# Handing buffers over between the stages of a graph network kernel: first attention started from the counting buffers

## The reference

```python
# layer 0: dot-product attention over the edges, 4 heads of 64
scores = sum(q[dst] * k[src]) / 8
alpha  = softmax of scores over the edges of each dst
x = layernorm(layernorm((segment_sum(alpha * v[src]) + skip) @ Wout + x) * g + b + x)
# layer 1: GAT, 4 heads, with self loops, then a feed-forward part
e = leaky_relu(al_src[src] + al_dst[dst], 0.2)
y = layernorm(x + segment_sum(softmax(e) * h[src])) * g1 + b1
x = layernorm(layernorm(y + gelu(y @ W1) @ W2) * g2 + b2 + x)
# layer 2: two rounds of x + segment_sum(relu(x)[src]), each with a two-layer MLP
# layer 3: a GCN sum with degree norms, then GAT attention with one head, layernorm
```

## Time and profile before

| what | value |
|---|---|
| median of 3 runs | 3881.09 us (3879.44 to 3882.41) |
| the profiled execution, as timed | 3878.65 us |
| its span | 3876.9 us |
| PE busy | 3705.8 us (96%) |
| DVE busy | 2282.5 us (59%) |
| ACT busy | 2042.2 us (53%) |
| POOL busy | 534.9 us (14%) |
| counting | up to about 509 us |
| first attention | about 509 to 1625 us |
| second attention | about 1625 to 2517 us |
| sums and last attention | from about 2517 us |

### The profile page before, as it was taken

One profiled execution on the slowest core, in us unless ns is written; L12 is line 12 of the kernel. 1 busy time (PEld: TensorE's weight loads), 2 busy tenths in 40 slices (PEclk: granted clock), 3 DMA queues, 4 the chain that ended last, 5 costly groups with the idle time before them and its releaser, 6 DMA issues. The chain is left out here.

```text
span 3876.9 us, 69921 instructions
## 1 busy us (share of the span) xinstructions
PE 3705.8 (96%) x27529; PEld 2886.1 (74%) x27530; DVE 2282.5 (59%) x4502; ACT 2042.2 (53%) x3736; POOL 534.9 (14%) x599
## 2 busy tenths in 40 slices
PE   6999969999999999699999999799999999999999
PEld 3666647677777676587777777688888888888887
DVE  8999936555655655499999999600012221005665
ACT  3555546666666666499999999600001110003554
POOL 1000000111111111100005667500000000000000
PEclk9999979999999999899999999999999999999999
DMA  2555572332333233533343333154343333334332
GB/s 95 226 229 210 237 243 85 110 112 91 114 99 104 91 115 104 145 132 116 120 173 104 113 113 111 60 211 147 129 145 138 138 137 126 136 120 144 138 138 72
DMA packets 177941, 520.61 MB, mean 134 GB/s; under 512 B 54385, under 2 KB 142454, under 8 KB 144502
## 3 DMA queue, kind: packets, MB, share of 16 engines
q1 hardware_dynamic: 175110, 509.49, 37.8%
q10 hardware_dynamic: 2544, 7.08, 0.6%
HBM read 354.22 MB, written 162.29 MB: 133 GB/s over the span
## 5 line engine op out<-in xcount | busy, mean ns | idle before, releaser
L1858 PE MATMUL t_acc<-t_r,t_ct 128*128 128x256 f32 (+1 forms) x3750 | 856.0, 380 | 20.0 <-DMA t_r<-d_r 16.2
L1036 ACT ACTIVATE a_sm<-a_p_t 128x1024 f32<-128x1024 f32 (+1 forms) x800 | 669.4, 837 | 372.9 <-PE a_p_t L974 356.6
L1858 PEld LDWEIGHTS t_acc<-t_r,t_ct 128*128 128x128 f32 x3750 | 701.4, 190 | 114.1 <-DMA t_r<-d_r 16.6
L974 PE MATMUL a_p_t<-ident,a_sm 128*128 128x128 f32 x5000 | 702.8, 280 | 36.6 <-ACT a_sm L1036 20.2
L1030 ACT ACTIVATE a_sm<-a_sm,a_negm 128x1024 f32<-128x1024 f32 (+2 forms) x600 | 703.1, 1172 | 43.1 <-DVE a_negm L1098 42.8
L974 PEld LDWEIGHTS a_p_t<-ident,a_sm 128*128 128x128 f32 x5000 | 562.5, 143 | 212.9 <-issue 194.1
L988 PE MATMUL a_p_o<-a_sm,a_v 128*64 128x128 f32 x10000 | 700.6, 279 | 10.2 <-ACT a_sumT L1043 9.1
L988 PEld LDWEIGHTS a_p_o<-a_sm,a_v 128*64 128x64 f32 x10000 | 555.8, 137 | 188.1 <-issue 109.9
L1118 DVE CUSTOM_DVE_ANT_0 a_sm<-a_p_s,sh_rows 128x400 f32<-128x400 f32 x800 | 427.2, 571 | 426.8 <-PE a_p_s L960 415.2
L960 PE MATMUL a_p_s<-sh_a_bc,a_q 64*128 64x400 f32 x1600 | 397.8, 557 | 27.7 <-DMA sh_rows<-d_logs 21.7
L1139 DVE SCALAR_TENSOR_TENSOR a_sm<-sh_a_bc,sh_al 128x3125 f32<-128x3125 f32 x100 | 346.2, 3462 | 15.0 <-PEq L52 11.6
(11 more groups left out here) (248 smaller groups left out, 3682.2 us busy)
## 6 DMA issues: line engine op xcount, KB each, us to landing
t_ct<-d_ct SPq DMA_DIRECT2D x74, 1600.0 KB, 6.6
sh_rows<-d_full SPq DMA_DIRECT2D x50, 1600.0 KB, 7.1
d_logs<-logs SPq DMA_DIRECT2D x25, 1664.0 KB, 7.0
sh_rows<-d_logs SPq DMA_DIRECT2D x25, 1664.0 KB
d_ct<-ct SPq DMA_DIRECT2D x25, 1600.0 KB, 5.3
d_full<-sh_rows SPq DMA_DIRECT2D x25, 1600.0 KB, 6.3
t_ct<-d_full SPq DMA_DIRECT2D x25, 1600.0 KB, 6.8
t_x<-d_x SPq DMA_DIRECT2D x75, 128.0 KB, 6.6
```

Source lines behind the costliest of these rows:

```text
L974: m = nc.tensor.transpose(p_t[u % 2][:, i * P:(i + 1) * P], sm[buf][:, a * P:(a + 1) * P], ident[:, :])
L1036: nc.scalar.activation(sm[buf][:, a_row[u] * P:a_row[u + 1] * P], p_t[u % 2][:, 0:turns[u] * P], ACT.Copy).then_inc(s_copy, 1)
L1858: m = self.nc.tensor.matmul(self.acc[t % 2][:, 0:width], self.ct[t % 3][:, a * P:(a + 1) * P], rows[:, a, 0:width], start=a == 0, stop=a = ...
```

## The change

- `Shared` is made once, ahead of counting, and holds one wide buffer. Counting writes its counts and edges there, the first attention has its keys there, the second its source terms, and the sums their messages, counts row 2 and weights. `logs` are the two `rows` of the attentions.
- The first attention takes its tiles in the order 23, 24, 0, 1, ... 22 (`tile_at`). The logarithms of tiles 23 and 24 aren't stored and loaded; they are used where counting left them. DVE masks those of tile 23 at the end of counting.
- SP loads the keys of the first 23 tiles (eight DMAs) and the query of tile 23 (four) in the last counting tile, ahead of the store of its counts, and the keys of the last two tiles (four DMAs) behind the loop. PE waits for them in the new block, not SP in the old one.
- The scores of the first two units go round three pairs of banks: `p_s` and the two transposition buffers. The first transposition waits until all of them are masked. ACT takes one exponential ahead of its first unit.
- The source terms of the first attention's last two tiles are stored in tiles 2 and 3 of the second attention. `hand_sources` loads its first part in two pieces.
- In `post_a1` the steps with g2 and be2 move from POOL to DVE. The relu of the last five tiles writes straight into the messages of the sums; messages of the first 20 tiles and counts rows 0 to 2 are loaded within the second attention, behind its last tile. The end of that block no longer waits for stores.

```diff
+def tile_at(j):
+    return (j + NT - 2) % NT
+KEPT = 20
...
+        wide = sb("wide", [P, MESSAGES + 2 * NPAD])
+        self.a_bc = wide[:, 0:4 * NPAD].rearrange("p (h k n) -> p h k n", h=2, k=2)
+        self.messages = wide[:, 0:MESSAGES].rearrange("p (a n) -> p a n", a=NT)
+        self.kt = wide[:, 2 * NPAD:4 * NPAD].rearrange("p (h n) -> p h n", h=H0)
...
-        ct = [sb(f"ct{i}", [P, NT, P], FP32) for i in range(2)]
-        logs = [sb(f"logs{i}", [P, ROW], FP32) for i in range(2)]
+        ct, logs = shared.counts, shared.rows
...
+                def hand_keys(a, b):
+                    proj.stored_keys(sp, b)
+                    for h in range(H0):
+                        rows = w_kt[(h % 2) * HD:(h % 2 + 1) * HD, h // 2, :, :].rearrange("p j n -> p (j n)")
+                        for r in range(2):
+                            lo, hi = max(a * P, r * HALF_K), min(b * P, (r + 1) * HALF_K)
+                            if lo < hi:
+                                sp.dma_start(shared.kt[r * HD:(r + 1) * HD, h, lo - r * HALF_K:hi - r * HALF_K], rows[:, lo:hi]).then_inc(shared.s_kt, 16)
...
+                    if last:
+                        hand_keys(0, NT - 2)
+                        proj.stored_keys(sp, NT - 1)
+                        hand_queries()
                     wait_alone(sp, s_group_out, (j + 1) * GPT)
...
-                store_logs(NT - 2, 1)
                 proj.store_vs(sp, NT - 1)
-                store_logs(NT - 1, 0)
+                hand_keys(NT - 2, NT)
...
+                dve.wait_ge(s_tbank_out, (NT - 1) * NTU)
+                for e in range(NFULL):
+                    v.scalar_tensor_tensor(logs[1][:, c], logs[1][:, c], STEEP, logs[1][:, c], ALU.mult, ALU.min).then_inc(shared.s_full, 1)
...
+        def score_bank(n, i):
+            if n >= len(first_units):
+                return p_s[i % 2][:, 0:SW]
+            pair = (n * SU + i) // 2 % RING
+            return p_s[i % 2][:, 0:SW] if pair == 0 else p_t[pair - 1][:, o:o + SW]
...
-                        freed = n * SU + i - 1
+                        freed = n * SU + i - (1 if n >= len(first_units) else 2 * RING - 1)
...
+                    if dot and n == 0 and u == 0:
+                        pe.wait_ge(s_sfree, len(first_units) * SU)
...
-                    P_.store(sp, NT - 2, 1, (NT - 2) // 2)
+                    P_.store_rows(sp, NT - 2, 1, (NT - 2) // 2)
+                    P_.store_values(sp, NT - 2, 1, (NT - 2) // 2)
...
+                    if p == 0 and j in (2, 3):
+                        sp.dma_start(al_src_dram[:, :, c * P:(c + 1) * P].rearrange("h k p -> p (h k)"), shared.as_[i][:, :], allow_slow_non_contiguous=True).then_inc(shared.s_terms[i], 16)
...
-                P_.stored(sp)
+                    if j == NT:
+                        sp.wait_ge(s_mask, units - heads)
+                        sp.dma_start(shared.rows[0][:, 0:NPAD], row(ct_dram, 0)).then_inc(shared.s_sum[0], 16)
+                        sp.wait_ge(s_lift, units)
+                        sp.dma_start(shared.messages[:, 0:KEPT, :], r2_dram[:, 0:KEPT, :]).then_inc(shared.s_messages, 16)
+                        sp.wait_ge(s_mask, units)
+                        sp.dma_start(shared.rows[1][:, 0:NPAD], row(ct_dram, 1)).then_inc(shared.s_sum[1], 16)
+                        sp.dma_start(shared.row2, row(ct_dram, 2)).then_inc(shared.s_sum[2], 16)
...
                 if (lag, s) == (4, 0):
+                    v.scalar_tensor_tensor(t[:, :], t[:, :], n2.mv[:, 0:1], rows["g2"][:, :], ALU.subtract, ALU.mult).then_inc(DL.sem, 1)
+                    dve.wait_ge(DL.sem, DL.at(jj, "gain2"))
                     dve.wait_ge(PL.sem, PL.at(jj, "rstd2"))
-                    v.tensor_scalar(z[:, :], t[:, :], n2.mv[:, 0:1], n2.rs[:, 0:1], ALU.subtract, ALU.mult).then_inc(DL.sem, 1)
+                    v.scalar_tensor_tensor(z[:, :], t[:, :], n2.rs[:, 0:1], rows["be2"][:, :], ALU.mult, ALU.add).then_inc(DL.sem, 1)
...
-                    pool.tensor_tensor(z[:, :], z[:, :], rows["g2"][:, :], ALU.mult).then_inc(PL.sem, 1)
-                    pool.tensor_tensor(z[:, :], z[:, :], rows["be2"][:, :], ALU.add).then_inc(PL.sem, 1)
...
+                    to = r2[tp] if jj < KEPT else messages[:, jj, :]
+                    nc.scalar.activation(to[:, 0:D], x2[tp][:, :], ACT.Relu).then_inc(AR.sem, 1)
...
-        for i in range(NT // PIECE):
-            a = i * PIECE
-            sp.dma_start(self.ct[0][:, a * P:(a + PIECE) * P], self.ct_dram[0, :, a * P:(a + PIECE) * P]).then_inc(self.s_first[i], 16)
-            sp.dma_start(self.r[0][:, a:a + PIECE, :], self.r2[:, a:a + PIECE, :]).then_inc(self.s_first[i], 16)
         load_x(0)
         gin_weights(0)
-        load_row(1)
-        load_row(2)
```

More of the change, by code:

```diff
@@ L702, in attend @@
         if dot:
-            full = shared.rows
-            kt = shared.a_bc[:, 1, :, :].rearrange("p k n -> p (k n)").rearrange("p (h n) -> p h n", h=heads)
-            q = [sb(f"q{i}", [P, heads, P]) for i in range(2)]
+            full = [shared.rows[1], shared.rows[0]]
+            kt, q = shared.kt, shared.q
             p_s = [pb(f"p_s{i}", [P, UNIT]) for i in range(2)]
         else:
-            mask = [shared.rows[1], shared.rows[0]]
+            mask = shared.rows
             a_bc, al = shared.a_bc, shared.al
@@ L713, in attend @@
         s_v = sem("values")
-        s_k = [sem(f"keys{h}") for h in range(heads)]
         s_src = [sem(f"source_terms{h}") for h in range(heads)]
@@ L1185, in _ @@
                     fill()
-                    for e in range(NFULL):
-                        mask_logs(0, 0, 0, e)
                 for at in first_units:
@@ L1500, in make @@
         zT = sb("zT", [P, 4, P])
-        x2 = [sb(f"x2{i}", [P, D]) for i in range(2)]
+        x2, messages, s_lift = shared.x2, shared.messages, scores
         r2 = [sb(f"r2{i}", [P, D + 1]) for i in range(2)]
@@ L1509, in make @@
         s_tin = [sem(f"post_in{i}") for i in range(2)]
-        s_out = [sem(f"post_stored{i}") for i in range(2)]
+        s_out = shared.s_x2
         s_init = sem("post_init")
@@ L1613, in dve @@
                     stats(dve, n3, z[:, :], DL, "3", jj)
+                if (lag, s) == (4, 5) and jj == KEPT:
+                    v.memset(messages[:, KEPT:NT, D:D + 1], 1.0)
                 if (lag, s) == (4, 5):
@@ L1698, in __init__ @@
         sem = semaphores(nc, ctx, "t_")
-        self.r = [sb("r0", [P, NT, D + 1]), sb("r1", [P, NT, D])]
-        self.ct = [sb(f"ct{i}", [P, NPAD]) for i in range(3)]
-        self.sm = [sb(f"sm{i}", [P, NPAD]) for i in range(2)]
+        self.r = [shared.messages, sb("r1", [P, NT, D])]
+        self.ct = [shared.rows[0][:, 0:NPAD], shared.rows[1][:, 0:NPAD], shared.row2]
+        self.sm = [sb("sm0", [P, NPAD]), shared.weights]
         self.a_bc = sb("a_bc", [P, 2, NPAD])
@@ L1786, in load_x @@
                 sp.wait_ge(self.DO.sem, self.DO.at(i - 2 * NT - 2, "relu"))
+            if t == KEPT:
+                for k in range(2):
+                    sp.wait_ge(self.shared.s_x2[k], rows_stored(NT - 1 - k))
             if t == SUMS:
```

252 lines of the change are left out of this document (141 added, 111 removed).

## The result

The changed kernel takes 3852.35 us (median of 4 runs, 3851.14 to 3853.03), the kernel before 3881.75 us beside it (4 runs, 3879.44 to 3884.26): ratio 0.992, 95% interval 0.9906 to 0.9938. That is 29.4 us less, where 44.2 were forecast (3836.9, range 3827 to 3849). Sign and order are right, the size is not: the time lies outside the range.

What follows compares the result with a forecast made beforehand. TensorE was busy 96% of the span, with three block-change waits over 16 us; DVE led the second attention's second pass. Gains 16.8 + 6.2 + 4.5 + 4.2 + 12.5 = 44.2 us off 3881.09 gave 3836.9 us, range 3827 to 3849.

Steps and rivals of the forecast that it cites:

- a steady stretch costed at nothing: First attention's steady state: no wait of weight on PE, no instruction touched by the change, so no gain or loss.
- the landing of the last keys' store: End of counting: the store issued at 494.15 lands 5.2 us later, at 499.4, before four key loads are issued.
- rival A: First attention's first scores: without gaps they bring the full clock early, 4.8 us more gain, 3832 us; chance 0.2.
- Part 1a: Hand-over from counting to first attention: PE's first score at 504.5 instead of 521.34, gain 16.8 us, bounds 13 and 18.5.
- Rival C: Last counting tile: key issues and loads not covered, up to 4 us ahead of the last stores, 3841 us; chance 0.07.
- near 5: Sign of being right: PE's wait before the first score near 5 us instead of 21.75.
- Part 1b: Scores of the first attention's first two units: three bank pairs at half clock take 14.7 us instead of 20.9, gain 6.2.
- part 1: Start of the first attention, hand-over and first two units' scores together: 23.0 us ahead at the first transposition.
- Part 2: Start of the second attention: slow source-term store no longer delays the x1b store, so ACT's end decides; gain 4.5 us.
- Part 3: Second attention's second pass: norm steps moved from POOL to DVE save 0.2 us a tile over 21 tiles, 4.2 us.
- Rival B: Second attention's second pass: DVE takes the port before POOL, 8.4 us lost where 4.2 were gained, 3849.5 us; chance 0.13.
- Part 4: Start of the sums: shorter post chain, no store or load in the way; gain 12.5 us, bounds 10 and 14.

Runs made afterwards that it cites:

- the run on keys: Changed kernel plus loop-start assertions, keys of tiles 0 to 19 handed over one counting tile earlier: 3836.3 us, ratio 0.988.
- 0.22 in the run: Changed kernel plus loop-start assertions, with gain and bias of the second attention's second layer norm back on POOL: 3849.1 us.

## Why the prediction was wrong

Two steps failed. The larger one, a steady stretch costed at nothing, took 16.5 us; the smaller one, the landing of the last keys' store, took 5.7 us. The second was hidden in part by luck: the scores gained 3.7 us more than forecast, by rival A, which I had not chosen.

**Part 1a, hand-over, 16.8 us forecast, 11.1 measured.** The step that failed: "such a store lands 5.2 us after issue, so at 499.4". The issues were covered, as worked out; what they issue was not. 3.0 MB of key loads go through the same engines at some 190 to 250 GB/s (issued from 484.24 on, those of 400 KB landed after 7.8 us), and the last stores stand behind the 1.3 MB that are left of them. Rival C had the mechanism and the wrong size, "up to 4 us" from issue times; measured 7.7 us on the store (12.9 against 5.2) and 5.7 on the start. The 5.2 us row was a single store, with the counts' store just ahead of it but no load in its way. The rest of the chain held: PE's wait was 10.98 us and is 4.66 in the run on keys, against "near 5".

**Part 1b, scores, 6.2 us forecast, 9.9 measured (20.9 against 10.9).** Rival A was right about the clock: gapless scores raised it from 0.50 to 1.00 within 8 us. I weighed the row (92% busy and half clock) as "the nearest row: the same instructions in the same place", and it wasn't near: its 8% are a gap in each round. Of the 9.9 us, 2.0 are still there with two banks (20.9 against 18.9, the masking that moved out of the stretch), the rest comes from the banks. Here the Trainium skill's sentence (TensorE: Matmul & The Clock Gate, section What's actually happening) that sustained activity releases the throttle agrees with the trace, where PE has no gap, and the run with two banks keeps 0.50 through 18.9 us. Then 1.1 us went back: PE waits 2.12 us for the last masking at 521.17, and the clock falls to 0.50 once more from 523 to 529. I had carried the wait at 1.1 us and no price for the clock behind it. From the first transposition on, part 1 stands at 19.9 of 23.0.

**The first attention's steady state, costed at nothing, -16.5 us.** This is the missing term. "The first attention in its steady state [...] the change touches no instruction there" was true and no ground for the zero: the stretch had hold-ups of up to 2.3 us a tile in the kernel before and up to 4.4 in the changed one, which the order of waits doesn't show (those of PE of over 0.35 us, between 540 and 1600, add to 4 us before and 12 after). The signs were in the trace of before: periods of 44.5, 43.0, 43.8 and 44.2 us beside fourteen of 42.2, and the earlier trace rows, where a 4-byte store delays what follows by 9 us. I had read that row for part 2, and asked of the moved stores only what stands behind them in one queue. Each tile of the attention has the same store. No rival held this, so the range was too narrow: had it carried 0 to 25 us of losses that come out anew with each build or execution, with 8 of them already in the time of before it would have reached 17 us up, to 3854. Why the changed kernel's profile has 16.5 us more of them than that of before is not known.

**Part 2, 4.5 us forecast, 5.5 measured**, of which 4.9 are the block change: DVE starts 1.07 us after ScalarE's end at 1615.64 (1.4 forecast), 5.95 before. The cause was named rightly; the run of the kernel before with 32-byte pieces shows that the 1024 pieces of 4 bytes are all of it.

**Part 3, 4.2 us forecast, 3.1 measured** between the lift of the second hand-over and the last step of the block (8.8 to 11.9), 0.16 us a tile (19.99 to 19.84), 0.22 in the run. POOL's root still comes late, by 0.53 us after the gain step and not 0.3, since the gain step runs while POOL waits; the addition shrank as forecast (0.62 to 0.29 us). Rival B, a loss, did not come:

```profile
2057.14 3.36 POOL L1616 TENSOR_SCALAR a_n_ve<-a_n_mv 128x1 f32<-128x1 f32 x1 [5.21 <-DVE a_n_mv L1611]
...
2060.34 0.48 DVE L1693 SCALAR_TENSOR_TENSOR a_t<-a_t,a_n_mv,a_g 128x256 f32<-128x256 f32 x1
...
2061.34 0.49 DVE L1696 SCALAR_TENSOR_TENSOR a_z<-a_t,a_n_rs,a_be 128x256 f32<-128x256 f32 x1 [0.53 <-POOL a_n_rs L1618]
```

POOL's first step (to 2060.50) overlaps the gain step by 0.16 us, so it isn't shut out a second time.

**Part 4, 12.5 us forecast, 13.4 measured** (11.9 to 25.3, at the first turn of the sums' result, 2540.91 against 2515.63): PE starts 1.1 us after the relu (1.4 forecast), no message and no count row is waited for, and the second row of sums follows the first.

Together: 42.1 us by the profiles without the hold-ups' 16.5, against 44.2. **Not settled:** by what path memory traffic holds up PE, DVE and ScalarE, which read and write only on-chip memory there. The clog itself is not enough. It is there in tiles that lose nothing as well, as in one of the run without query loads that took 42.21 us (713.3 to 720.3, again 2 to 9 us after the post step):

```profile
q1 hardware_dynamic: 21, 0.28, 76.0%
```

That is 4.1 us for a piece of 13 KB. A late supply of instructions doesn't explain the worst tile: in the changed kernel no piece of an instruction queue runs from 1263.9 to 1278.9. What PE did is open too. In the worst tile its matmuls are recorded without a gap up to 1273.46, while the signals of five groups of them, recorded as ended between 1269.81 and 1273.46, reach their semaphores only between 1274.72 and 1275.01; so either PE stood still, with its ends modelled too early, or its signals came late. Its only recorded wait there, 1.92 us, comes after that. The clock is no witness for the rest: between 640 and 1560 us it falls in this one tile of the changed kernel and in none of the kernel before. Over the 22 tiles (columns as above; the changed kernel, then the one with 32-byte pieces) PE is idle for 15.0 and 3.5 us, and the other half of the loss is recorded as longer busy time:

```profile
622.97:1576.42 953.45, 938.42 (x8451) 659.60 (x8450) 550.00 (x1933) 637.62 (x1189) 127.92 (x199) 1.00 0.33 102
```

```profile
627.22:1555.84 928.62, 925.11 (x8451) 653.90 (x8450) 549.42 (x1933) 642.16 (x1189) 128.43 (x199) 1.00 0.29 105
```

Nor was it tried why the losses differ so much between builds, or whether they differ between chips.

## What to carry to other kernels

Before costing a steady stretch at nothing, list its periods tile by tile: if some are longer than the rest in one place, there is a term that can come out otherwise in another build or execution, and the range must hold it. In this kernel a store of many tiny pieces was paid by whatever came in the 10 us after it, so look at what precedes a slow transfer and not only at the transfer; gather such values and turn them once. And when issues are moved into a covered place, cost the transfers that they start against the stores that stand behind them, not only the queue's issue time.

## What was new about the hardware

- 1024 stores of 4 bytes took the DMA engines 1.5 us and slowed all traffic of the core for about 9 us after: pieces of 13 KB took 4.2 us on average instead of 0.5. Stores of the same 4 KB in 128 pieces of 32 bytes, in another order, had no such wake.
- With such stores, engines that touch no main memory there waited longer in some tiles: DVE up to 4.6 us at once, and a tile took up to 4.4 us more; without them no tile did. The path is not known.
- Scores of 64 rows in depth raised the granted clock from 0.50 to 1.00 within 8 us when nothing lay between them, and left it at 0.50 for 18.9 us with a gap of 0.18 us in every 2.37.
- A tile with two fp32 matmuls more, of 4 stationary columns and 128 moving ones, took 0.68 us more where PE leads.
